# Macaron block on one core: whole turns of a step's phase counted by ScalarE, and a new order of stages

## The reference, cut to what matters

```python
x = x + 0.5 * ffn(layernorm(x))     # 8 experts of width 256, the best 2 for each row, and a shared expert of width 512
x = x + attn(layernorm(x))
x = x + 0.5 * ffn(layernorm(x))

# inside attn, for each of 32 x 8 = 256 channels and 8 angles theta:
phi = k_val[..., None] * theta
re_k, im_k = jnp.cos(phi), jnp.sin(phi)
cs = jnp.cumsum(p_w * (re_k, im_k), axis=1)        # along the 512 rows
out_re = sum(state_re * q_re + state_im * q_im)    # over the 8 angles
out_im = sum(state_im * q_re - state_re * q_im)
```

## Time and profile before

| | us |
|---|---|
| median of 3 runs | 1239.68 (1239.1 to 1245.08) |
| the profiled execution | 1235.89 |
| its span in the trace | 1234.6 |
| busy in it: PE (TensorE matmul) | 970.2 |
| DVE (VectorE) | 719.1 |
| ACT (ScalarE) | 586.2 |
| POOL (GpSimd) | 441.7 |

### The profile page before, as it was taken

How to read it: one execution, slowest core, us unless ns; L and a number is a source line. 1 busy time by engine, 2 the same in 40 slices (tenths; PEclk the granted TensorE clock), 3 DMA queues, 4 the chain that set the end, 5 groups by cost and what they waited for, 6 DMA issues and landing times.

```text
span 1234.6 us, 10515 instructions
## 1 busy us (share of the span) xinstructions
PE 970.2 (79%) x3168; PEld 525.8 (43%) x3168; DVE 719.1 (58%) x1162; ACT 586.2 (47%) x1008; POOL 441.7 (36%) x424
## 2 busy tenths in 40 slices
PE   5899999944979888967935376798987897679993
PEld 2446664412435454523412133355454443336661
DVE  3400001277988998886898878799987961200000
ACT  4424444324536687656333254367668841314441
POOL 4154553003633363252000235427263301165552
PEclk9999999975989899987977777999998999799997
DMA  8965666336436776874233672348567553125666
GB/s 286 378 240 104 118 111 108 75 86 153 107 105 140 164 162 133 183 169 114 83 104 71 169 188 69 94 136 182 104 163 174 101 135 60 45 62 110 111 111 102
DMA packets 65227, 164.05 MB, mean 133 GB/s; under 512 B 11314, under 2 KB 11314, under 8 KB 63062
## 3 DMA queue, kind: packets, MB, share of 16 engines
q0 software_dynamic: 29440, 65.10, 30.0%
q1 hardware_dynamic: 35734, 98.30, 26.3%
HBM read 108.13 MB, written 63.60 MB: 139 GB/s over the span
## 4 chain that ended last, share of the span: by engine, by line
PE 46%; DVE 15%; DMA 12%; ACT 12%; POOL 7%; issue 7%; SPq 1%; POOLq 0%; DVEq 0%; ACTq 0%
PE yps L845 10%; PE hps L829 9%; PE hps L776 7%; PE yps L788 6%; PE misc L907 6%; POOL slots L1578 4%; DVE run L1395 2%; DMA outT<-tail_sb 2%; DMA x_rows<-tail_sb 2%; PE misc L873 2%; DMA x_rows<-ys,rows_i 2%; ACT xin L1045 2%; DVE trig L1402 1%; DMA q_cols<-xin 1%; PE misc L864 1%
## 5 line engine op out<-in xcount | busy, mean ns | idle before, releaser
L845 PE MATMUL yps<-w_all,hidden_sb 128*128 x368 | 180.8, 614 | 32.7 <-ACT hidden_sb L1010 32.7
L829 PE MATMUL hps<-w_all,hidden_sb 128*128 x736 | 176.5, 383 | 4.2 <-ACT hidden_sb L993 4.2
L829 PEld LDWEIGHTS hps<-w_all,hidden_sb 128*128 128x128 f32 x736 | 138.7, 192 | 52.6 <-issue 38.0
L1395 DVE TENSOR_TENSOR_SCAN run<-pwx,trig 128x512 f32<-128x512 f32 x128 | 149.3, 1207 | 19.0 <-ACT trig L1095 18.5
L1590 POOL DMA_INDIRECT xs<-x_normal,rows_i x92 | 107.5, 1168 | 137.2 <-PE xps L820 105.3
L776 PE MATMUL hps<-xnT,sw_sb 128*128 128x512 f32 x256 | 122.3, 627 | 4.8 <-ACT xnT L961 2.7
L788 PE MATMUL yps<-sw_sb,hidden_sb 128*128 128x512 f32 x256 | 120.4, 614 | 0.0
L1614 POOL DMA_INDIRECT x_rows<-ys,rows_i x48 | 82.4, 1717 | 72.3 <-ACT ys L1023 67.4
L845 PEld LDWEIGHTS yps<-w_all,hidden_sb 128*128 128x128 f32 x368 | 67.7, 194 | 95.1 <-issue 93.0
L1023 ACT ACTIVATE ys<-yps,slots 128x512 f32<-128x512 f32 x92 | 63.3, 688 | 88.4 <-PE yps L845 83.1
L1578 POOL DMA_INDIRECT slots<-told,dest_i x64 | 76.9, 1201 | 58.5 <-DVE cmp_a L1264 30.0
(11 more groups left out here) (201 smaller groups left out, 1592.4 us busy)
## 6 DMA issues: line engine op xcount, KB each, us to landing
qx<-q_cols SPq DMA_DIRECT2D x128, 256.0 KB
x_normal<-xin SPq DMA_DIRECT2D x32, 256.0 KB, 5.3
w_all<-in_w_experts SPq DMA_DIRECT2D x8, 1024.0 KB, 8.0
xin<-x_rows SPq DMA_DIRECT2D x32, 256.0 KB, 5.0
turns_sb<-in_w_out SPq DMA_DIRECT2D x3, 1536.0 KB, 9.9
xin<-in_x SPq DMA_DIRECT2D x16, 256.0 KB, 4.4
sum_rows<-ys SPq DMA_DIRECT2D x16, 256.0 KB, 3.0
xin<-sum_rows POOLq DMA_DIRECT2D x16, 256.0 KB, 8.9
```

The source lines that it names most:

```text
L829: t = PE.matmul(hps[:, bank, 0:H], xT[:, j % 2, c, :], w_all[:, bass.ds(expert[j] + c * H, H)], start=c == 0, stop=c == KC - 1)
L845: t = PE.matmul(yps[:, bank, :], hb[:, j % 2, ec, :], w_all[:, bass.ds(expert[j] + (KC * H + ec * D), D)], start=ec == 0, stop=ec == EC - 1)
L1395: t = VE.tensor_tensor_scan(run[:, c, :], pwx[:, n // M, :], trig[:, n % 2, c, :], 0.0, ALU.mult, ALU.add)
```

## The change

A new stage `c_int` on ScalarE makes the whole turns: an ACTIVATE with Copy, a scale per partition and an int32 output, into the same place of `trig`. It waits for what L1382 waited for (the sums of step i - 2, and the kept channel). L1382 is gone from VectorE; the instruction behind it (L1384 before, L1394 now) waits for ScalarE. In the planner's table the new stage stands with 0.7 us, VectorE's `c_turn` falls from 1.3 to 0.8 us, and other lengths are changed; so all five lists come out in another order. Behind the first changed lines the line numbers of the changed kernel are 1 to 15 higher than those before.

```diff
-            piece("POOL", ("load", q), 4.6, ("DVE", ("load", q)))
-            piece("ACT", ("norm", q), 2.4, ("POOL", ("load", q)))
+            piece("POOL", ("load", q), 3.6, ("DVE", ("load", q)))
+            piece("ACT", ("norm", q), 3.0, ("POOL", ("load", q)))
...
-                piece("PE", s, 0.7 if j % AT_ONCE else 1.9, ("POOL", ("bring", g, j), 3.3),
+                piece("PE", s, 0.6 if j % AT_ONCE else 1.3, ("POOL", ("bring", g, j), 3.3),
...
-                piece("PE", s, 1.9, ("ACT", ("mid", g, j)), bank=[("yps", ("ACT", s))])
+                piece("PE", s, 1.8, ("ACT", ("mid", g, j)), bank=[("yps", ("ACT", s))])
...
-            piece("DVE", ("c_turn", b, n), 1.3, ("DVE", ("a_mem", b, half)), *free, *([] if i else [("DVE", ("w_soft", 1))]))
+            piece("ACT", ("c_int", b, n), 0.7, ("DVE", ("a_mem", b, half)), *free, *([] if i else [("DVE", ("w_soft", 1))]))
+            piece("DVE", ("c_turn", b, n), 0.8, ("ACT", ("c_int", b, n)))
...
+            def count_turns(b, n):
+
+                half, m = divmod(n, M)
+                if b > 0 or n >= 2:
+                    last = STEPS_OF[STEPS_OF.index((b, n)) - 2]
+                    act.wait_ge(*(out_summed if last[1] % M else added).at((*last, 0)))
+                act.wait_ge(*convolved.at((b, half, CW - 1)))
+                if (b, n) == (0, 0):
+                    act.wait_ge(*weighing.at(21))
+                SE.activation(trig_int[:, n % 2, 0, :], kept(b, half), ACT.Copy,
+                              scale=theta_sb[:, half, m:m + 1]).then_inc(*turns_counted.of((b, n)))
...
-                if b > 0 or n >= 2:
-                    last = (b, n - 2) if n >= 2 else (b - 1, STEPS + n - 2)
-                    vec.wait_ge(*(out_summed if last[1] % M else added).at((*last, 0)))
-                vec.wait_ge(*convolved.at((b, half, CW - 1)))
-                VE.tensor_scalar(trig_int[:, s, 0, :], kept(b, half), th, None, ALU.mult).then_inc(*phase_int.of((b, n)))
-                vec.wait_ge(*phase_int.at((b, n)))
+                vec.wait_ge(*turns_counted.at((b, n)))
                 VE.scalar_tensor_tensor(trig[:, s, 1, :], kept(b, half), th, trig_int[:, s, 0, :],
                                         ALU.mult, ALU.subtract).then_inc(*phase_made.of((b, n)))
```

More of the change, by code:

```diff
@@ L291, in plan_weights @@
             piece("SP", ("w_bias",), 0.9, ("DVE", ("w_bias",)))
-            piece("POOL", ("w_rest",), 13.0, ("POOL", ("load", 0)))
+            piece("POOL", ("w_rest",), 9.0, ("POOL", ("load", 0)))
             piece("SP", ("w_rest",), 3.6, ("POOL", ("w_rest",)))
@@ L309, in plan_job @@
             piece("DVE", ("load", q), 3.4, ("SP", ("fetch", q), 3.6))
-            piece("POOL", ("load", q), 4.6, ("DVE", ("load", q)))
-            piece("ACT", ("norm", q), 2.4, ("POOL", ("load", q)))
-            piece("SP", ("norm", q), 1.8, ("ACT", ("norm", q)))
+            piece("POOL", ("load", q), 3.6, ("DVE", ("load", q)))
+            piece("ACT", ("norm", q), 3.0, ("POOL", ("load", q)))
+            piece("SP", ("norm", q), 2.4, ("ACT", ("norm", q), -2.1))
             for tb in range(TB):
                 s = ("turn", q, tb)
-                piece("PE", s, 0.7, ("ACT", ("norm", q)), *turned_rows, bank=[("xps", ("ACT", s))])
+                piece("PE", s, 0.7, ("ACT", ("norm", q), -0.7 * (TB - 1 - tb)), *turned_rows, bank=[("xps", ("ACT", s))])
                 piece("ACT", s, 0.6, ("PE", s))
@@ L330, in plan_job @@
                 s = ("hidden", q, n)
-                piece("PE", s, 3.7, *kept_rows, *start[:1], *blocks_end, bank=[("hps", ("ACT", s))])
+                piece("PE", s, 3.6, *kept_rows, *start[:1], *blocks_end, bank=[("hps", ("ACT", s))])
                 piece("ACT", s, 0.7, ("PE", s), *([("PE", ("acc", q - 1, TB - 1))] if q else []), table="gelu")
@@ L368, in plan_blocks @@
                 s = ("one", g, j)
-                piece("PE", s, 1.9, ("ACT", ("x", g, j)),
+                piece("PE", s, 1.8, ("ACT", ("x", g, j)),
                       *([("SP", ("w_expert", E - 1), 10.0)] if g == 0 else []), bank=[("hps", ("ACT", ("mid", g, j)))])
@@ L401, in plan_head @@
             piece("DVE", ("a_stats", b), 3.4, *[("POOL", ("a_add", b, tb), 3.8 - 0.8 * (TB - 1 - tb)) for tb in range(TB)])
-            piece("POOL", ("a_stats", b), 4.6, ("DVE", ("a_stats", b)))
-            piece("ACT", ("a_norm", b), 2.4, ("POOL", ("a_stats", b)))
+            piece("POOL", ("a_stats", b), 3.6, ("DVE", ("a_stats", b)))
+            piece("ACT", ("a_norm", b), 3.0, ("POOL", ("a_stats", b)))
             for tb in range(TB):
                 s = ("a_turn", b, tb)
-                piece("PE", s, 0.7, ("ACT", ("a_norm", b)), *turned_rows, bank=[("misc", ("ACT", s))])
+                piece("PE", s, 0.7, ("ACT", ("a_norm", b), -0.7 * (TB - 1 - tb)), *turned_rows, bank=[("misc", ("ACT", s))])
                 piece("ACT", s, 0.6, ("PE", s))
@@ L601, in macaron @@
         pwx_made = signal("s_pwx", staged("a_spread", "ACT"))
+        turns_counted = signal("s_turns_counted", staged("c_int", "ACT"))
         abs_made = signal("s_abs", staged("c_turn", "ACT"))
@@ L618, in macaron @@
         den_made = signal("s_den", [(b, i) for b in range(B) for i in range(4)])
-        phase_int = signal("s_phase_int", staged("c_turn", "DVE"))
         phase_made = signal("s_phase", staged("c_turn", "DVE"))
@@ L1142, in scalar_program @@
                     keep_falls(*at)
+                elif stage == "c_int":
+                    count_turns(*at)
                 elif stage == "c_turn":
```

## The result

The changed kernel is **slower by 2.2%**: 1268.58 us median (1262.58 to 1270.98, 4 runs) against 1240.41 of the kernel before beside it, ratio 1.0222 [1.0181, 1.0263]. The forecast was 1227 us, with a range of 1207 to 1247. The profiled execution took 1270.16 us, its span is 1268.9.

The account below looks back on a forecast made before the run. DVE was taken to pace the steps in two stretches, with a chain of rows and slots setting stretch 2 and PE ending stretch 3. Terms -12.1, -1 and +0.4 gave -12.7 us, from 1239.7 to 1227 us, range 1207 to 1247.

Parts of the forecast that it names:

- stretch 1: 250 to 653 us, 32 steps to the end of batch 1, held to end when DVE ends; forecast -12.1 us.
- stretch 2: 653 to 790 us, 12 steps, a chain from output rows to slots that DVE waits for; forecast -1 us.
- stretch 3: 790 to 1045.5 us, 20 steps to the end of the output rows, ending on PE; forecast +0.4 us.
- The instruction removed: L1382 on DVE: 0.50 us a step, 32 us over 64 steps, the most the edit itself can give.
- Stretches 1 and 3, what the removal is worth: Removal at 0.50 us a step: -16.0 us in stretch 1, 10 us gained by DVE in stretch 3.
- rival 2: PE and ACT, not DVE, set the stretches, so the removal becomes waits: -4 us, 1236 us; chance 0.2.
- The instruction added: Count on ACT at 0.71 us, 45 us, plus 18 table loads, 23 us: ACT from 586 to about 655 us.
- the two stretches beside the blocks: Windows beside groups 1 and 2, 187 and 195 us: ACT was to be busy for 159 and 155 us.
- The wait added: DVE waiting for ACT's count, with 2.1 us to spare each step: 9 to 10 us over all.
- rival 3: Counts come late beside the blocks, 1.1 us a step: +17 us, 1257 us; deciding mean wait 0.50; chance 0.18.
- Stretch 3's order: Last two blocks' Gelus stand behind the waves of step (3, 15), so job 6's `hidden` begins 6.2 us later.
- The rest: 189 us behind the output rows stay as they are; PE's wait of 30 us ending stretch 1 stays too.

Follow-up runs that it names:

- e2: Kernel before with only the count moved from VectorE to ACT, order and lengths of before: ratio 1.0206 to the kernel before.
- e19: e2 plus a stop: VectorE's phase instruction waits for the end of the scans ahead of it: ratio 1.0001 to the kernel before.
- e16: Changed kernel plus a stop: VectorE's phase instruction waits for the end of the scans ahead of it: ratio 1.0131 to the kernel before.
- e9: Changed kernel plus an unneeded 64-column product on VectorE ahead of each phase and a wait for its end: ratio 1.0103 to the kernel before.
- e18: e8 plus a stop: VectorE's phase instruction waits for the end of the scans ahead of it: ratio 0.9953 to the kernel before.
- e1: Changed kernel's order alone, the product in whole turns given back to VectorE: ratio 1.0152 to the kernel before.
- e12: e9 with the phase planned at 1.5 us instead of 0.8, order redrawn: 1246.37 us, ratio 1.0062 to the kernel before.
- e15: Changed kernel redrawn with the count a step early in its own buffer, longer planned phase and short 64-column product: ratio 1.0248 to the kernel before.
- e8: Kernel before without the count on any engine or the wait for its end, waves scaled to nearly nothing: ratio 1.0132 to the kernel before.
- e3: Changed kernel's code, count planned as an ACT stage, all other planned lengths those of the kernel before: ratio 1.0228 to the kernel before.
- e13: e8 plus a 64-column product of two SBUF inputs ahead of each phase and a wait for its end: ratio 0.9969 to the kernel before.
- e6: e2 with the count in a one-byte buffer of its own, so made a step earlier: ratio 1.0247 to the kernel before.

## Why the prediction was wrong, by its own steps

By stretch, from one execution of each kernel: stretch 1 was forecast at -12.1 us and came out at +7.2 (3.5 of them there before the first scan), stretch 2 at -1 and +10.8, stretch 3 at +0.4 and +16.6.

**The instruction removed:** DVE's busy time fell by 28.7 us, about the 30.3 of its row; that part is right. The step that failed here is the price: L1382 was counted as time on DVE alone, and what else hung on it stood at nothing, without a reason. The phase's wait for its end was the stop in a step's row behind which a standing indirect DMA of POOL got through. Without it such instructions cost 25 us in the old order (e2 against e19) and 11 to 15 in the new one (changed kernel against e16 and e9). No rival held this, and none of the rows shows POOL's indirect DMAs.

**Stretches 1 and 3, what the removal is worth:** mis-sized. Less DVE work with nothing against it brought 5.8 us in all (e18), not the 16 of stretch 1 and 10 of stretch 3. A row without gaps made me take VectorE for the pace; it is the pace only until the next wave or block is late. That was rival 2, whose 4 us are about right for this term. The time itself rose, which rival 2 doesn't say.

**The instruction added:** 719 ns for 710, ACT 650 us for 655, 121 loads. Right, although the two stretches beside the blocks got less of it than reckoned (ACT busy for 145 and 137 us, not 159 and 155).

**The wait added:** the sum said 9 to 10 us; in the changed kernel it is 17.9, with 24.5 more before the scans. In the old order 28.3 us, 0.44 us a step, bring the time back to that of the kernel before (e19). That is near rival 3's deciding point of 0.50, but by luck: both sides of it came through at about a fifth, as 28.3 us of waits took back the 5.8 us that 32 us of removal had brought. Its lateness came, and so did its direction; the order and POOL's standing, which cost more, are not in it.

**Stretch 3's order:** +0.4 forecast; +11.2 with the order alone (e1) and +16.6 in the changed kernel. `hidden` of job 6 came at 1020.6, not 973, and 1007.7 with the order alone (e1). My step let the Gelus of the last two blocks fall behind the waves of (3, 15), and then let PE begin 8.3 us later; but the last blocks are a chain of Gelu, matmuls and Gelu, and PE waits for ACT in it (8.01 us before the row at 1006.96) and then runs at a granted clock of 0.50 for 3.5 us. Over the whole kernel PE's matmuls take 21.4 us more with the order alone (991.6 us, e1); how much of the order's cost that is, or only follows from its waits, no run separates. That the plan's steps go by too fast, and so put the blocks behind too many of them, is borne out at the end by e12, which plans the phase longer; that it is all of the order's cost isn't shown.

**Stretch 2:** -1 forecast, and -1.2 with the removal alone (e18, 651.3 to 783.5 against 650.6 to 784.0); +11 with the order (e1), which the sum did not reckon with in this stretch. Which stage of the order costs it stays open.

**The rest:** the stretch behind the output rows stayed as it was. The 29.97 us that PE waited behind batch 1 didn't stay: PE had other work in it and waits 6.10 us there.

In sum, by the ratios: the new order +19 us (e1), the count in place of the product, with POOL's way open, -3 (e16 against e1) to -6 (e9 against e1, both within the intervals), POOL's standing +11 to +15. That makes up the 28 us between the medians.

## What to carry to other kernels

An instruction of VectorE that you take away may have been the gap that another engine used. Before you count its time as gain, look at POOL's indirect DMAs beside it; if the row then runs without a break, try one wait for an end that is due anyway. A list of stages that a planner drew is an operating point of its own: all kernels here with a redrawn list came out 0.6 to 2.5% slower, also those in which POOL's way was open (e1, e9, e12, e15). So measure the edit in the old order first, and the new order without the edit.

## What the runs showed of the hardware

In the traces VectorE's successive instructions overlap by some 0.07 us, and as long as they do, an indirect DMA instruction of POOL can stand for 19.53 us in place of 0.96 (e8; 24.01 in e3). A stop of 0.03 to 0.11 us in VectorE's row was followed by the end of a standing slots instruction 0.4 to 0.9 us later, whatever instruction was near (the product before, two inputs in e13, none in e16). Some also ended without a stop, after up to 7.88 us (e2, changed kernel). Behind 8.01 us of waiting PE's four matmuls took 3.78 us at a granted clock of 0.50, and 1.98 us at 1.00. ACT's Copy with a scale per partition took 719 ns for int32 (changed kernel) and 706 for int8 output (e6), 128 x 512; VectorE's product took 473 ns for 512 columns and still 240 for 64 (e9).
